# Two transformer layers on one core: the bias of the MLP's first product made by ScalarE, and another order of steps in a turn

## The chip, the core and the metric
The kernel runs on one core of a Trainium2 chip. Its time is the device time in microseconds of one execution; the median of three is 1187.67 us.

## The reference
An input x (2048 tokens of width 256, 32 sequences of 64) goes through four blocks, all in fp32:

```
x = offset_attention(x, ctx)
for layer in (1, 2):
    x += self_attention(layernorm(x))            # 16 heads of 16
    x += cross_attention(layernorm(x), ctx)
    x += gelu(layernorm(x) @ w1 + b1) @ w2 + b2  # w1: 256 x 1024
x = recurrent_block(x, state)
```
The change lies in the two layers.

## The kernel before
The tokens are cut into 4 groups of 512, each of 4 tiles of 128 tokens (2 sequences). The two layers are 8 **turns** (TURNS = 2 layers x 4 groups). A turn n works on 8 attention tiles k, 0 to 3 self-attention and 4 to 7 cross-attention of group n, and in the gaps on the MLP of the turn before (`prev`) and on the entry of the next one (`nxt`: layernorm, queries, keys, values). Turn 0 has no `prev`, turn 7 no `nxt`; 1 to 6 are one loop body. Each engine has a `turn` function of its own, a list written out by hand; an engine runs its list strictly in order, and semaphores join the engines.

One tile k goes like this. TensorE: `scores` (L976). VectorE: `mask`, a product with the mask (L1349). GpSimd: `add_mask` (L787). VectorE: `maximum` (L1356), `subtract` (L1361). ScalarE: `exps` (L1207). TensorE: `probs_T`, 8 transposes (L986). ScalarE: `copy_pT` (L1212). TensorE: `times_v` (L1001). VectorE: `normalize` (L1367, L1369). TensorE: `result_T` (L1009). ScalarE: `copy_cT` (L1217). TensorE: `out_project` (L1022). VectorE: `residual` with the layernorm's statistics (L1378 to L1385). GpSimd: `inv_std` (L792). VectorE: `norm` (L1390). Names with `next_` are one or two tiles ahead, names with `last_` one behind.

The MLP: `norm_T_mlp` (TensorE, L913), `norm_out(2)` (ScalarE, L1172), eight `hidden(j)` (TensorE, 512 wide, L1039) into two PSUM banks in turn, `pre(j)`, which adds b1 and empties the bank (VectorE, L1407), `gelu` in two halves of four (ScalarE, L1225), four `mlp_out(p)` (TensorE, L1053), `result(p)` (VectorE, L1399). `hidden(j)` for j from 2 to 5 waits for `pre(j - 2)`. The middle layernorm of a tile: `norm_T_mid` (L900), `norm_out_mid` (L1180), `queries_mid` (L957, L1192). Cross keys and values: `keys_ctx` and the entry's queries and keys (L870), `keys` (ScalarE, L1200), `values_ctx` and `values_in` (L880), `values` (VectorE, L1332). The entry: `stats_in` and `norm_in` (VectorE, L1308 to L1323), `queries_in` (ScalarE, L1187). `add_bias` and `add_bias_in` (GpSimd, L764 to L780) add row biases; `cross_masks` (L1340) prepares the masks.

SyncE's list holds the loads and stores. The x load of turn n + 2 waits for `add_bias_in` and `norm_in` of turn n + 1, and in turns 2 to 4 the second layer's weights are loaded in the same list, in parts, as the first layer's come free: the middle set (cross-attention's keys, values and queries) stands behind the x load in turn 3.

## Time and profile before

| what | value |
|---|---|
| median of 3 runs | 1187.67 us (1187.09 to 1188.38) |
| the profiled execution | 1188.55 us, span 1186.8 us |
| TensorE busy | 1050.7 us, 89% |
| VectorE busy | 815.3 us, 69% |
| ScalarE busy | 509.0 us, 43% |
| GpSimd busy | 434.1 us, 37% |
| mean granted clock | 0.961 |

Busy shares are of the whole span; the two layers take from about 110 to 819 us of it. A busy TensorE has matmuls in flight, at the clock then granted (1 is 2.4 GHz, 0.5 is 1.2 GHz). In the groups below, "idle before" is the time in which an engine stood before such an instruction, and the arrow names whose result ended it.

### The profile page before, as it was taken

Reading aid. Unit: us, or ns where it says so; the run is one execution under the profiler, and the core shown is the slowest. Engines: PE = TensorE matmul, PEld = TensorE weight load, DVE = VectorE, ACT = ScalarE, POOL = GpSimd, SP = SyncE. Lnnn points to the kernel's source line nnn. Section 1 sums busy time; section 2 is a strip of 40 time slices with the busy share of each in tenths; the row PEclk is TensorE's granted clock in tenths of the full one; section 3 lists DMA queues with packets and bytes.
Section 4 is the critical chain, followed back from the end, with each engine's and each line's share of the span. In section 5 each row is a group of like instructions: output and inputs, shape, how many; then the busy total and the mean of one; then the engine's idle time right before and its main releaser. Section 6 shows DMA issues by size and latency. Waiting matters only on the chain. (4 is left out here: it accounts for less than half of the span.)

```text
span 1186.8 us, 23743 instructions
## 1 busy us (share of the span) xinstructions
PE 1050.7 (89%) x9056; PEld 714.6 (60%) x9056; DVE 815.3 (69%) x1573; ACT 509.0 (43%) x954; POOL 434.1 (37%) x387
## 2 busy tenths in 40 slices
PE   7988786999999999999999999978996988888866
PEld 5876565668668668668668668656363353443524
DVE  3654776776776776776776866862448787796864
ACT  4643353464364363363373373461231434414331
POOL 2111443442442442442343343331307427264250
PEclk9988888999999999999999999989998999999988
DMA  7130100001002002102101000030000010010100
GB/s 252 62 94 23 41 1 19 24 2 38 24 2 74 23 2 82 36 2 77 55 6 33 24 18 20 9 115 18 1 27 30 1 36 21 0 38 0 36 1 18
DMA packets 38005, 41.14 MB, mean 35 GB/s; under 512 B 8640, under 2 KB 33536, under 8 KB 37648
## 3 DMA queue, kind: packets, MB, share of 16 engines
q1 hardware_dynamic: 37776, 39.54, 10.5%
q8 instruction: 82, 1.34, 0.5%
q14 instruction: 19, 0.16, 0.0%
q0 software_dynamic: 128, 0.10, 0.0%
HBM read 31.25 MB, written 8.39 MB: 33 GB/s over the span
## 5 line engine op out<-in xcount | busy, mean ns | idle before, releaser
L1356 DVE TENSOR_REDUCE b_neg_max<-head_area 128x16 f32<-128x1024 f32 x64 | 77.9, 1218 | 113.9 <-POOL head_area L787 113.5
L2104 POOL TENSOR_TENSOR c_rs<-c_st,head_area 128x512 f32<-128x512 f32 x64 | 88.6, 1416 | 96.8 <-DVE c_st L2583 95.9
L792 POOL TENSOR_TENSOR b_rstd<-b_var,minus_half 128x1 f32<-128x1 f32 x63 | 34.5, 548 | 241.4 <-DVE b_var L1385 241.4
L1207 ACT ACTIVATE head_area<-head_area 128x1024 f32<-128x1024 f32 x64 | 67.9, 1060 | 112.3 <-DVE head_area L1361 111.7
L1039 PE MATMUL ps<-b_hT_mlp,wl 128*128 128x512 f32 x224 | 108.3, 606 | 8.7 <-DVE b_act_g L1407 8.6
L1053 PE MATMUL ps<-w,b_act_g 128*128 128x256 f32 x448 | 104.4, 387 | 2.9 <-ACT b_act_g L1225 2.9
L787 POOL TENSOR_TENSOR head_area<-head_area,b_self_add 128x1024 f32<-128x1024 f32 x32 | 76.7, 2396 | 80.0 <-DVE head_area L1349 80.0
L787 POOL TENSOR_TENSOR head_area<-head_area 128x1024 f32<-128x1024 f32 x32 | 75.5, 2359 | 75.7 <-DVE head_area L1349 75.7
L1212 ACT ACTIVATE head_area<-ps 128x512 f32<-128x512 f32 x128 | 69.9, 598 | 72.5 <-PE ps L986 72.5
L1053 PEld LDWEIGHTS ps<-w,b_act_g 128*128 128x128 f32 x448 | 84.2, 193 | 15.6 <-ACT b_act_g L1225 3.0
L870 PE MATMUL ps<-head_area,wl 128*128 128x512 f32 x176 | 85.5, 609 | 0.0
L986 PE MATMUL ps<-ident,head_area 128*128 128x128 f32 x512 | 72.1, 287 | 12.7 <-DVE head_area L1349 11.8
L1361 DVE TENSOR_TENSOR head_area<-head_area,b_neg_max 128x1024 f32<-128x1024 f32 x64 | 78.1, 1220 | 1.2
L2583 DVE TENSOR_TENSOR_SCAN c_st<-head_area,ps 128x512 f32<-128x512 f32 x64 | 73.6, 1201 | 2.8 <-ACT ps L2391 2.8
L986 PEld LDWEIGHTS ps<-ident,head_area 128*128 128x128 f32 x512 | 60.6, 147 | 23.5 <-DVE head_area L1349 14.0
L1022 PE MATMUL ps<-wl,b_cT 128*128 128x256 f32 x252 | 70.1, 403 | 1.4 <-ACT head_area L1192 1.4
L1039 PEld LDWEIGHTS ps<-b_hT_mlp,wl 128*128 128x128 f32 x224 | 38.7, 190 | 45.7 <-issue 27.5
L1217 ACT ACTIVATE b_cT<-ps 128x256 f32<-128x256 f32 x64 | 24.5, 383 | 96.5 <-PE ps L1009 96.5
L880 PE MATMUL ps<-wl,head_area 128*64 128x128 f32 x1024 | 65.1, 282 | 0.0
L880 PEld LDWEIGHTS ps<-wl,head_area 128*64 128x64 f32 x1024 | 57.6, 141 | 9.1 <-issue 9.1
L1022 PEld LDWEIGHTS ps<-wl,b_cT 128*128 128x128 f32 x252 | 46.6, 201 | 13.9 <-issue 6.7
L870 PEld LDWEIGHTS ps<-head_area,wl 128*128 128x128 f32 x176 | 31.6, 193 | 24.9 <-issue 24.1
(262 smaller groups left out, 2213.1 us busy)
## 6 DMA issues: line engine op xcount, KB each, us to landing
head_area<-x_mid SPq DMA_DIRECT2D x9, 512.0 KB, 3.8
wl<-in_wl SPq DMA_DIRECT2D x4, 1024.0 KB, 6.8
head_area<-in_ctxT SPq DMA_DIRECT2D x8, 512.0 KB, 3.6
x_mid<-b_x_out SPq DMA_DIRECT2D x8, 512.0 KB, 3.6
area<-in_wc SPq DMA_DIRECT2D x1, 2336.0 KB, 8.5
a_x_in<-in_x SPq DMA_DIRECT2D x16, 128.0 KB, 2.9
a_y_in<-in_ctx SPq DMA_DIRECT2D x16, 128.0 KB, 3.4
w<-in_w SPq DMA_DIRECT2D x2, 1024.0 KB, 9.4
```

The lines of the kernel that those rows point to most:

```text
L787: pool.tensor_tensor(t, t, m.unsqueeze(1).broadcast_to([P, NH, S]), ALU.add).then_inc(add_ok, 1)
L870: mm = pe.matmul(ps[:, YB + c, :], weight(name, k, first + c * P, first + (c + 1) * P), rhs[:, k, :], start=(k == 0), stop=(k == NC - 1))
L880: mm = pe.matmul(ps[odd * S:(odd + 1) * S, YB + half, b * P:(b + 1) * P], lhs[:, k, t:t + S], weight(name, k, odd * P, (odd + 1) * P), sta ...
L986: mm = pe.transpose(ps[:, PT + half, i * P:(i + 1) * P], sc[:, k % 2, half, 2 * i:2 * i + 2, :].rearrange("q i k -> q (i k)"), w["ident"][ ...
L1022: mm = pe.matmul(ps[:, CO, OUT], cT[:, half, p * P:(p + 1) * P], weight(("ao", "co")[a], half), start=(half == 0), stop=(half == 1))
L1039: mm = pe.matmul(ps[:, YB + j % 2, :], weight("w1", k, j * P, (j + 1) * P), hT_mlp[:, k, :], start=(k == 0), stop=(k == NC - 1))
L1053: mm = pe.matmul(ps[:, YB + MLP_BANK[p], 0:D], act_g[:, j, p * P:(p + 1) * P], w["w2"][:, j, :], start=(j == 0), stop=(j == NJ - 1))
L1212: act.activation(pT[:, b, :, :].rearrange("k i q -> k (i q)"), ps[:, PT + b, :], ACT.Copy).then_inc(pT_ok, 1)
L1356: dve.tensor_reduce(neg_max[:, k % 2, :], t, AX, ALU.max, negate=True).then_inc(max_ok, 1)
L1361: dve.tensor_tensor(t, t, neg_max[:, k % 2, :].unsqueeze(2).broadcast_to([P, 2 * NPAIR, S]), ALU.add).then_inc(sub_ok, 1)
L2104: pool.tensor_tensor(rs[:, i % BUFS, :], st[:, i % 3, :], rF[:, i // RS, :], ALU.mult).then_inc(rs_ok, 1)
L2583: dve.tensor_tensor_scan(st[:, i % 3, :], decay[:, i // RS, :, :].rearrange("f b t -> f (b t)"), ps[:, VB[i % 4], :], 0.0, ALU.mult, ALU.a ...
```

## The change
`pre` goes from VectorE's list to ScalarE's, as an Identity activation with the bias; all four `turn` lists are put in another order. No other instruction is written in or taken out.

```diff
--- before.py
+++ after.py
@@ -812,41 +812,41 @@
             def turn(n, prev, nxt, entry_of=None):
                 last_inv_std(n, 0, prev)
+                add_bias(prev, 6)
                 next_add_mask(n, 0, nxt)
-                add_bias(prev, 6)
                 last_inv_std(n, 1, prev)
-                inv_std_in(nxt if entry_of is None else entry_of)
+                add_bias_in(nxt, 0)
                 next_add_mask(n, 1, nxt)
                 add_bias(prev, 7)
+                inv_std_in(nxt if entry_of is None else entry_of)
                 last_inv_std(n, 2, prev)
+                add_bias_in(nxt, 1)
                 next_add_mask(n, 2, nxt)
-                add_bias(n, 0)
-                add_bias_in(nxt, 0)
+                add_bias_in(nxt, 2)
                 last_inv_std(n, 3, prev)
                 next_add_mask(n, 3, nxt)
+                add_bias(n, 0)
                 add_bias(n, 1)
-                add_bias_in(nxt, 1)
                 last_inv_std(n, 4, prev)
                 next_add_mask(n, 4, nxt)
                 add_bias(n, 2)
-                add_bias_in(nxt, 2)
+                add_bias(n, 3)
+                next_add_mask(n, 5, nxt)
                 last_inv_std(n, 5, prev)
-                next_add_mask(n, 5, nxt)
-                add_bias(n, 3)
-                add_bias_in(nxt, 3)
-
-                last_inv_std(n, 6, prev)
                 next_add_mask(n, 6, nxt)
                 add_bias(n, 4)
+                last_inv_std(n, 6, prev)
+                add_bias_in(nxt, 3)
+
                 last_inv_std(n, 7, prev)
+                add_bias(n, 5)
                 next_add_mask(n, 7, nxt)
-                add_bias(n, 5)
             add_mask(0, 0)
             add_mask(0, 1)
@@ -1068,39 +1068,40 @@
             def turn(n, prev, nxt):
+                keys_ctx(n, 0, prev)
+
                 probs_T(n, 0, nxt)
                 last_project(n, 0, prev)
-                keys_ctx(n, 0, prev)
                 times_v(n, 0)
                 next_scores(n, 0, nxt)
                 keys_ctx(n, 1, prev)
                 result_T(n, 0)
                 values_ctx(n, 0)
+                last_project(n, 1, prev)
                 probs_T(n, 1, nxt)
-                last_project(n, 1, prev)
                 values_ctx(n, 1)
                 times_v(n, 1)
                 next_scores(n, 1, nxt)
                 norm_T_mlp(prev, n)
+                norm_T_mid(n, 0)
                 result_T(n, 1)
-                norm_T_mid(n, 0)
                 hidden(prev, 0, nxt)
                 queries_mid(n, 0)
                 probs_T(n, 2, nxt)
                 last_project(n, 2, prev)
-                hidden(prev, 1, nxt)
                 times_v(n, 2)
                 next_scores(n, 2, nxt)
+                hidden(prev, 1, nxt)
                 hidden(prev, 2, nxt)
-                hidden(prev, 3, nxt)
                 result_T(n, 2)
                 norm_T_mid(n, 1)
-
-                probs_T(n, 3, nxt)
+                hidden(prev, 3, nxt)
                 queries_mid(n, 1)
                 hidden(prev, 4, nxt)
+
+                probs_T(n, 3, nxt)
                 last_project(n, 3, prev)
                 times_v(n, 3)
                 next_scores(n, 3, nxt)
@@ -1108,45 +1109,45 @@
                 result_T(n, 3)
                 norm_T_mid(n, 2)
                 norm_T_in(nxt, prev)
+
                 probs_T(n, 4, nxt)
-
                 queries_mid(n, 2)
                 queries_in(nxt, 0)
                 last_project(n, 4, prev)
                 times_v(n, 4)
                 next_scores(n, 4, nxt)
                 queries_in(nxt, 1)
+                keys_in(nxt, 0)
+                norm_T_mid(n, 3)
+
+                probs_T(n, 5, nxt)
                 result_T(n, 4)
-                norm_T_mid(n, 3)
-                keys_in(nxt, 0)
+                keys_in(nxt, 1)
                 queries_mid(n, 3)
-
-                probs_T(n, 5, nxt)
-                last_project(n, 5, prev)
-                keys_in(nxt, 1)
+                hidden(prev, 6, nxt)
                 times_v(n, 5)
                 next_scores(n, 5, nxt)
-                hidden(prev, 6, nxt)
+                hidden(prev, 7, nxt)
+                last_project(n, 5, prev)
                 result_T(n, 5)
-                hidden(prev, 7, nxt)
                 probs_T(n, 6, nxt)
-                last_project(n, 6, prev)
                 values_in(nxt, 0, prev)
                 times_v(n, 6)
                 next_scores(n, 6, nxt)
+                last_project(n, 6, prev)
+                result_T(n, 6)
                 mlp_out(prev, 0, nxt)
-                result_T(n, 6)
+
+                probs_T(n, 7, nxt)
                 mlp_out(prev, 1, nxt)
-
-                probs_T(n, 7, nxt)
                 last_project(n, 7, prev)
+                times_v(n, 7)
                 values_in(nxt, 1, prev)
-                times_v(n, 7)
                 next_scores(n, 7, nxt)
                 mlp_out(prev, 2, nxt)
+                mlp_out(prev, 3, nxt)
                 result_T(n, 7)
-                mlp_out(prev, 3, nxt)
             scores(0, 0)
             for half in range(2):
@@ -1216,6 +1217,14 @@
                 act.wait_ge(c_ps, tile(n, k) + 1)
                 act.activation(cT[:, :, p * P:(p + 1) * P], ps[:, CX, CT].rearrange("f (h q) -> f h q", h=2), ACT.Copy).then_inc(c_ok, 1)
+            def pre(n, j):
+                if n is None:
+                    return
+                if j == 0:
+                    act.wait_ge(ready["hidden"], n + 1)
+                act.wait_ge(hid_ps, NJ * n + j + 1)
+                act.activation(act_g[:, j, :], ps[:, YB + j % 2, :], ACT.Identity, bias=vec("b1", j)).then_inc(pre_ok, 1)
+
             def gelu(n, half):
                 if n is None:
                     return
@@ -1233,52 +1242,60 @@
             def turn(n, prev, nxt):
                 copy_pT(n, 0)
+                keys(1, n, 0)
+                keys(1, n, 1)
+                copy_cT(n, 0)
                 next_exps(n, 0, nxt)
-                keys(1, n, 0)
-                copy_cT(n, 0)
-                keys(1, n, 1)
                 copy_pT(n, 1)
-                next_exps(n, 1, nxt)
                 norm_out(2, prev)
                 norm_out_mid(n, 0)
                 copy_cT(n, 1)
-
+                next_exps(n, 1, nxt)
                 queries_mid(n, 0)
+
                 copy_pT(n, 2)
+                pre(prev, 0)
+                pre(prev, 1)
+                norm_out_mid(n, 1)
+                pre(prev, 2)
+                pre(prev, 3)
+                copy_cT(n, 2)
                 next_exps(n, 2, nxt)
-                norm_out_mid(n, 1)
-                copy_cT(n, 2)
-
                 queries_mid(n, 1)
+
                 copy_pT(n, 3)
                 next_exps(n, 3, nxt)
-                gelu(prev, 0)
+                pre(prev, 4)
+                pre(prev, 5)
                 norm_out_mid(n, 2)
+                norm_out(0, nxt)
                 copy_cT(n, 3)
-                norm_out(0, nxt)
-
                 queries_mid(n, 2)
+
                 copy_pT(n, 4)
+                next_exps(n, 4, nxt)
                 queries_in(nxt, 0)
-                next_exps(n, 4, nxt)
                 queries_in(nxt, 1)
+                keys(0, nxt, 0)
                 norm_out_mid(n, 3)
                 copy_cT(n, 4)
+                copy_pT(n, 5)
                 queries_mid(n, 3)
-                copy_pT(n, 5)
-                keys(0, nxt, 0)
+                keys(0, nxt, 1)
                 next_exps(n, 5, nxt)
-                keys(0, nxt, 1)
+                gelu(prev, 0)
+                pre(prev, 6)
                 copy_cT(n, 5)
+                pre(prev, 7)
                 copy_pT(n, 6)
                 gelu(prev, 1)
                 next_exps(n, 6, nxt)
+
+                copy_pT(n, 7)
                 copy_cT(n, 6)
-
-                copy_pT(n, 7)
                 next_exps(n, 7, nxt)
                 copy_cT(n, 7)
@@ -1398,14 +1415,6 @@
                 dve.wait_ge(bias_ok[2], NP * n + p + 1)
                 dve.tensor_tensor(x_out[:, p, :], ps[:, YB + MLP_BANK[p], 0:D], x_mlp[:, p, :], ALU.add).then_inc(out_ok, 1)
-            def pre(n, j):
-                if n is None:
-                    return
-                if j == 0:
-                    dve.wait_ge(ready["hidden"], n + 1)
-                dve.wait_ge(hid_ps, NJ * n + j + 1)
-                dve.tensor_scalar(act_g[:, j, :], ps[:, YB + j % 2, :], vec("b1", j), None, ALU.add).then_inc(pre_ok, 1)
-
             def next_maximum(n, k, nxt):
                 if k + 1 < TILES:
                     maximum(n, k + 1)
@@ -1438,79 +1447,72 @@
             def turn(n, prev, nxt, entry_of=None):
-                next_maximum(n, 0, nxt)
-                next_subtract(n, 0, nxt)
+                cross_masks(n)
                 last_residual(n, 0, prev)
                 normalize(n, 0)
+
+                next_maximum(n, 0, nxt)
                 last_norm(n, 0, prev)
+                next_subtract(n, 0, nxt)
                 next_mask(n, 0, nxt)
-                cross_masks(n)
+                values(1, n, 0)
+                last_residual(n, 1, prev)
                 next_maximum(n, 1, nxt)
-                values(1, n, 0)
+                values(1, n, 1)
+                last_norm(n, 1, prev)
+                normalize(n, 1)
                 next_subtract(n, 1, nxt)
-                last_residual(n, 1, prev)
-                values(1, n, 1)
-                normalize(n, 1)
-                last_norm(n, 1, prev)
                 next_mask(n, 1, nxt)
                 stats_in(nxt if entry_of is None else entry_of)
+                last_residual(n, 2, prev)
+                next_mask(n, 2, nxt)
+                last_norm(n, 2, prev)
+                normalize(n, 2)
                 next_maximum(n, 2, nxt)
-                pre(prev, 0)
                 next_subtract(n, 2, nxt)
-                last_residual(n, 2, prev)
-                pre(prev, 1)
-                normalize(n, 2)
-                last_norm(n, 2, prev)
-                next_mask(n, 2, nxt)
-                pre(prev, 2)
+
+                next_maximum(n, 3, nxt)
                 norm_in(nxt if entry_of is None else entry_of)
-
-                next_maximum(n, 3, nxt)
-                pre(prev, 3)
                 next_subtract(n, 3, nxt)
                 last_residual(n, 3, prev)
-                pre(prev, 4)
                 normalize(n, 3)
                 last_norm(n, 3, prev)
-                pre(prev, 5)
                 next_mask(n, 3, nxt)
                 next_maximum(n, 4, nxt)
                 next_subtract(n, 4, nxt)
                 last_residual(n, 4, prev)
+                next_mask(n, 4, nxt)
+                last_norm(n, 4, prev)
                 normalize(n, 4)
-                last_norm(n, 4, prev)
-                next_mask(n, 4, nxt)
                 next_maximum(n, 5, nxt)
                 next_subtract(n, 5, nxt)
+                normalize(n, 5)
+                next_mask(n, 5, nxt)
                 last_residual(n, 5, prev)
-                normalize(n, 5)
-                last_norm(n, 5, prev)
-                next_mask(n, 5, nxt)
-                pre(prev, 6)
                 next_maximum(n, 6, nxt)
-                pre(prev, 7)
                 next_subtract(n, 6, nxt)
-                last_residual(n, 6, prev)
-                last_norm(n, 6, prev)
-                values(0, nxt, 0)
                 normalize(n, 6)
                 next_mask(n, 6, nxt)
+                values(0, nxt, 0)
                 result(prev, 0)
+                last_residual(n, 6, prev)
+                result(prev, 1)
                 next_maximum(n, 7, nxt)
-                result(prev, 1)
+                last_residual(n, 7, prev)
                 next_subtract(n, 7, nxt)
-                last_residual(n, 7, prev)
-                last_norm(n, 7, prev)
+                normalize(n, 7)
                 values(0, nxt, 1)
-                normalize(n, 7)
                 next_mask(n, 7, nxt)
                 result(prev, 2)
+                last_norm(n, 5, prev)
+                last_norm(n, 6, prev)
+                last_norm(n, 7, prev)
                 result(prev, 3)
             dve.wait_ge(ready["first"], 1)
```

## Rows read from the trace of the kernel before

**Rows 1.** Windows: length, busy us of PE, PEld, DVE, ACT, POOL, clock, DMA.
```profile
110.23:202.07 91.84, 72.08 (x948) 56.04 (x949) 65.76 (x119) 34.37 (x61) 36.23 (x31) 0.83 0.07 21
...
291.87:380.24 88.37, 84.11 (x929) 61.08 (x929) 63.54 (x128) 43.38 (x68) 32.73 (x29) 1.00 0.11 33
...
732.16:819.32 87.16, 76.94 (x778) 56.19 (x776) 56.25 (x120) 37.06 (x59) 25.32 (x24) 0.94 0.15 49
202.07:732.16 530.09, 505.72 (x5568) 367.84 (x5569) 381.22 (x761) 259.97 (x408) 199.41 (x176) 1.00 0.09 29
```

**Rows 2.** Waits of PE, turns 1 to 6: total, times, longest.
```profile
PE ps L1039 <- DVE b_act_g L1407: 7.6, 12, 1.1
PE ps L1009 <- DVE head_area L1369: 7.5, 6, 1.3
PE ps L913 <- DVE head_area L1332: 4.9, 6, 0.8
PE ps L986 <- DVE head_area L1349: 3.6, 7, 0.8
```

**Rows 3.** Groups by form, one turn (307.97 to 396.33): busy us, mean ns, idle before.
```profile
L1356 DVE TENSOR_REDUCE b_neg_max<-head_area 128x16 f32<-128x1024 f32 x8 | 9.7, 1218 | 13.9 <-POOL head_area L787 13.8
L1407 DVE TENSOR_SCALAR b_act_g<-ps,vl 128x512 f32<-128x512 f32 x8 | 5.9, 743 | 0.4 <-PE ps L1039 0.4
...
L1212 ACT ACTIVATE head_area<-ps 128x512 f32<-128x512 f32 x16 | 8.7, 598 | 10.1 <-PE ps L986 10.1
L1207 ACT ACTIVATE head_area<-head_area 128x1024 f32<-128x1024 f32 x8 | 8.5, 1061 | 11.5 <-DVE head_area L1361 11.4
...
L1225 ACT ACT_TABLE_LOAD x2 | 2.6, 1283 | 0.0
L1207 ACT ACT_TABLE_LOAD x2 | 2.6, 1283 | 0.0
...
L1187 ACT ACTIVATE area<-ps,vl 128x512 f32<-128x512 f32 x2 | 1.4, 687 | 1.5 <-PE ps L870 1.4
```

**Rows 4.** Waits of PE, turn 0.
```profile
PE ps L1009 <- DVE head_area L1369: 10.5, 6, 3.9
PE ps L986 <- DVE head_area L1349: 6.8, 4, 4.6
```

**Rows 5.** Waits of PE, turn 7.
```profile
PE ps L1053 <- ACT b_act_g L1225: 2.9, 1, 2.9
```

**Rows 6.** Timeline of PE, start of turn 2: start, length, instruction.
```profile
291.87 1.09 PE L986 MATMUL ps<-ident,head_area 128*128 128x128 f32 x8 [0.42 <-issue]
292.80 1.03 PE L1022 MATMUL ps<-wl,b_cT 128*128 128x256 f32 x4
293.66 1.88 PE L870 MATMUL ps<-head_area,wl 128*128 128x512 f32 x4
295.47 1.13 PE L1001 MATMUL ps<-area,head_area 128*64 128x34 f32 x32
296.53 0.69 PE L976 MATMUL ps<-area 32*64 32x128 f32 x32
```

**Rows 7.** Timeline of GpSimd and VectorE, turn 2.
```profile
322.68 2.36 POOL L787 TENSOR_TENSOR head_area<-head_area 128x1024 f32<-128x1024 f32 x1 [2.23 <-DVE head_area L1349]
...
323.17 3.80 DVE L1323 TENSOR_SCALAR xc_in<-head_area,mv_in,rstd_in 128x256 f32<-128x256 f32 x4
```

**Rows 8.** Timeline of VectorE, tiles 6 and 7 of turn 0.
```profile
183.60 1.22 DVE L1356 TENSOR_REDUCE b_neg_max<-head_area 128x16 f32<-128x1024 f32 x1 [2.47 <-POOL head_area L787]
...
190.32 1.21 DVE L1349 TENSOR_TENSOR head_area<-ps,b_self_mul 128x1024 f32<-128x1024 f32 x1
194.00 1.22 DVE L1356 TENSOR_REDUCE b_neg_max<-head_area 128x16 f32<-128x1024 f32 x1 [2.47 <-POOL head_area L787]
```

**Rows 9.** Timeline of SyncE, turn 3.
```profile
445.44 0.37 SPq L680 DMA_DIRECT2D wl<-in_wl  x1
```

**Rows 10.** Windows: ten us of turn 0.
```profile
150.00:160.00 10.00, 7.85 (x44) 6.17 (x44) 9.77 (x15) 3.79 (x9) 4.46 (x4) 0.51 0.00 0
```

## The prediction, made before the change was measured

> **What bounds the kernel.** I read the windows of the two-layer stage first, turn by turn. A turn is the work between two starts of TensorE's transposes of tile 0. Six of the eight turns (1 to 6) are alike: together 530.09 us, TensorE busy 505.72 us of it at granted clock 1.00, VectorE 381, ScalarE 260, GpSimd 199; one of them is 88.37 us with TensorE busy for 84.11 [rows 1]. So TensorE bounds these turns, and what a new order can win in them is at most its idle time, 24.4 us or 4.1 us a turn. Turn 0, which has no MLP to fill holes, is different: 91.84 us, TensorE busy 72.08, mean clock 0.83. Turn 7, with no next group, takes 87.16 us with 76.94 busy at 0.94 [rows 1]. The stages before and after (the first 110 us, and the last 367) are not touched.
>
> Then TensorE's waits, to see who ends them. In turns 1 to 6 all are for VectorE [rows 2]: hidden products for the bias `pre` (7.6 us, 12 times), `result_T` for `normalize` (7.5), `norm_T_mlp` for the second `values` (4.9), `probs_T` for the mask product (3.6). VectorE isn't full; it is late because it works in program order and stands still elsewhere: 13.9 us of a turn it waits in front of `maximum` for GpSimd's `add_mask` [rows 3]. Nothing waits for ScalarE there. In turn 0 the waits are 10.5 us for `normalize` and 6.8 us for masks, one of them 4.6 us [rows 4]; in turn 7 the longest is 2.9 us for the second gelu [rows 5].
>
> **Bias to ScalarE.** Per turn 8 operations of 743 ns leave VectorE, 5.9 us. ScalarE's form of the same work is its Identity with a bias on the same 128x512, 687 ns, so it gains 8 x 0.69 = 5.5 us [rows 3]. ScalarE goes from 43.4 us busy in 88.4 [rows 1] to 48.9, less what follows. The row is the same kind of operation with the same shape, so both bounds of the price are close: 0.69, or 0.74 if it is no better than VectorE. The Trainium skill ("ScalarE: Activation LUTs", rules for kernel authors) says to put an add on VectorE and not on ScalarE. By that rule the move would be a loss on the unit cost. Here the source is PSUM in fp32 and the rows have ScalarE 0.06 us cheaper; the sum goes by the rows.
>
> **Two table loads less.** Before, exps stand between the two gelus, so a turn has 2 + 2 loads of 1283 ns [rows 3]. After, `gelu(prev, 0)` and `gelu(prev, 1)` have only Identity and Copy between them, which take no load in the kernel before when they follow a gelu. That leaves 1 + 1, and gives back 2.6 us of ScalarE: net +2.9 us, about 46 us busy a turn (52%). The same page (what a table load costs) puts 1.38 us of draining beside each load, 2.66 us a switch, so 5.3 us given back by it; the rows show the load alone, and ScalarE isn't the bound either way.
>
> **The order, walked through a steady turn.** I laid the new lists beside each other with start-to-start lengths from TensorE's rows [rows 6]: `probs_T` 0.93, a projection 0.86 to 0.95, `times_v` 1.06, `scores` 0.65, a 512-wide product 1.8; VectorE's large operations 1.2, exp 1.06, two `copy_pT` 1.1 to 1.2 [rows 3]; a residual with its statistics 1.3 and `add_mask` 2.4, both estimates from the loop in [rows 8]. Time 0 is the start of `keys_ctx(n, 0)`.
> - Head. `keys_ctx(0)` to 1.7 covers the last mask product and exp; `probs_T(0)` to 2.7, projection 3.6, `times_v(0)` 4.7, scores 5.3, `keys_ctx(1)` 7.0. VectorE: `residual(n, 7)` now comes first and waits until 3.8, `normalize(0)` is done at 5.8, well ahead of `result_T(0)`; `maximum(1)` and `subtract(1)` end at 8.6. ScalarE: `keys(1, n, 1)` waits until 7.1 with `copy_cT(0)` and exp of tile 1 queued behind it, done at 10.0. TensorE gets to `probs_T(1)` at 10.1. No stall, but the slack is 0.1 us.
> - The MLP's entry. `values(1, n, 1)` is done at about 15.0; `norm_T_mlp` begins at 14.7 and needs it at 15.1. The 0.8 us stall of before goes. `hidden(0)` waits for the second `norm_out` until about 16.7: a new stall of 0.5.
> - Hidden products. `pre(0)` is done at 21.8, `hidden(2)` is reached at 24.7; `pre(1)` at 25.5, `hidden(3)` at 26.9; likewise for 4 and 5. The 1.3 us a turn behind `pre` goes.
> - Middle. `norm_in` moves to where GpSimd rests. Before, its four operations took 3.80 us, beside an `add_mask` that began just before it [rows 7]; undisturbed I take 1.7. `normalize(3)` is done at 35.2 and `result_T(3)` is reached at 36.6: 1.25 us goes. Mask of tile 5 is done at 36.9, `probs_T(4)` is reached at 37.9: 0.5 goes.
> - End. Exp of tile 6 to 55.2, load and gelu to 58.4, `pre(6)` to 59.1: `values_in(0)`, reached at 58.9, waits 0.3. The second gelu ends at 63.3, `mlp_out(0)` is reached at 64.05. VectorE waits for `mlp_out` results with slack.
>
> Left are some 1.0 us of new stalls and small latencies; I take 1.1 against 4.1 us, **3.0 us a turn, 18 us for six turns**. Bounds: all idle gone, 24; half kept, 12; none, 0.
>
> **Turn 0.** In its last tiles VectorE runs a strict loop: maximum, subtract, residual, norm, values, normalize, mask, then GpSimd's addition before the next maximum. Two maxima stand 10.40 us apart, with the mask's start 6.72 us after the first; after the mask VectorE stands 2.47 us for the addition [rows 8]. The new order puts `normalize` and the mask ahead of residual and values, so these run beside the addition: 1.2 + 1.2 + 0.7 + 1.2 + 2.4 = 6.8 us, and then other chains (projection, copies, values) hold it near 8. Walking on from the first scores, `keys_ctx(0)` fills 1.8 us of the 4.6 us hole; `probs_T(2)` comes 3 us earlier than before, `probs_T(4)` 6 us, turn 1's tile 0 12 us, and then `keys_ctx` is already done. I take **13 us**. Bounds: 20, the idle time of the window (19.8), and 5, the opening and one tile. The clock's missing 0.17 I leave as it is.
>
> **Turn 7.** 10.2 us idle and some cold products. The same cures apply up to tile 5 (about 3 us of stalls); the shorter chain at tiles 4 to 6 wins 3 to 4. Against it, the chain exp, gelu, `pre(6)`, copies, gelu still has 8 us in a row on ScalarE, and `mlp_out(0)` keeps a stall of 2 to 3 us. `result_T(7)` is now last, so its copy (0.4 us) is no longer covered before all engines meet, +0.3. My walk ends 8 us earlier: **8 us**, bounds 3 and 11.
>
> **Queues.** SyncE's list is unchanged but what it waits for moves. `add_bias_in(nxt, 3)` goes behind `inv_std(n, 5)` on GpSimd, at about 70.6 of the turn. In turn 3 the x load and then the middle weights of layer 2 wait behind it. Before, the weights' first load was issued at 445.44 [rows 9], and turn 4 begins at about 468.5 (380.24 + 88.3) [rows 1]: 23 us. After, it is issued at about 71.5 of a turn of 85; a load of this kind I take at 8 us, so some 5 us of slack are left, and the first product of turn 4 now needs these weights. I cost it at nothing; if it slips it costs the slip once. `cross_masks` is earlier, the mask load with it: no cost.
>
> **Sum.** The profiled execution took 1188.55 us, its span is 1186.8, and the median of the runs is 1187.67, 0.9 lower. 1188.55 - 18 - 13 - 8 + 0.3 = 1149.9; by the median **1149 us**, 3.2% less.
>
> **Rivals.**
> - *The stalls only move* (chance 0.2). ScalarE's list now has in-order waits for TensorE (keys, `pre(1)`, `pre(3)`, `pre(5)`) with exps behind them; the 0.1 us of slack at `probs_T(1)` speaks for it, ScalarE's load of 52% to 55% against it. Steady turns keep 3 of 4.1 us and turns 0 and 7 give 14: 1187.67 - 6 x 1.1 - 14 = 1167.
> - *TensorE full everywhere* (0.1): 24 + 18 + 10 gone: 1136.
> - *Slower* (0.03): one mechanism, exp behind `keys(1, n, 1)` and the `pre`s. Each of the eight tiles would wait longer for its exp on TensorE. Turns 0 and 7 give 14 to 21 anyway, so it decides from a wait of 4.1 + 18/6 = 7.1 us a turn, 0.9 us for each tile. At 1.3 us a tile, 10.4 a turn, it gives 1187.67 + 6 x 6.3 - 18 = 1207.5. Against it: no wait for ScalarE in [rows 2], and 1.1 us in my walk.
> - *The change does nothing to measure* (0.03): the removed VectorE time was never on the path, and turn 0 is held by something the waits don't name: 1186 to 1190.
> - *The clock falls* (0.04). In 10 us of turn 0 with transposes, short products and small holes the granted clock was 0.51, near its lower level of 1.2 GHz, though TensorE was busy for 7.85 us [rows 10]. Turn 0's work at the full level is about 72.08 x 0.83 = 60 us; if the new order held it at a mean of 0.6 it would take 100 us, with 6 idle 106, so 14 us more than before instead of 13 less: 1187.67 - 18 - 8 + 14 = 1176. [...] Against it: fewer and shorter holes, and stretches of the same turn at 1.00.
>
> **Chances.** Forecast 0.6, the others as said. A measurement of this kernel can tell 0.2% from none. Faster 0.94, same 0.03, slower 0.03. The range takes the bounds of the three terms together with the first two rivals: 1136 to 1168.
>
> **What would show it.** TensorE's waits for the bias at `hidden` gone, and no other of over 0.5 us a turn in turns 1 to 6; a steady turn of 85 to 85.8 us; 7 + 7 table loads where there were 14 + 14; `norm_in` near 1.7 us; VectorE near 58 us a turn, ScalarE 46; turn 0 near 79 us and turn 7 near 79. Wrong would be waits of TensorE for exp above 1 us a turn, or a steady turn over 87.

## The result, and the profile after

After the change the kernel takes 1134.25 us (median of 4 runs, 1130.38 to 1135.84), against 1187.38 us before (4 runs, 1185.45 to 1188.38): ratio 0.955, 95% interval 0.9523 to 0.9577. The forecast was 1149 with a range from 1136 to 1168: the sign is right, the size too small, and the result lies 2 us outside the range. The profiled execution took 1134.52 us, 54.0 less than the profiled one of before.

The head of its page:

```profile
span 1132.7 us, 23729 instructions
...
PE 1030.0 (91%) x9056; PEld 707.2 (62%) x9056; DVE 768.0 (68%) x1517; ACT 517.4 (46%) x996; POOL 440.2 (39%) x387
```

TensorE's busy time fell from 1050.7 to 1030.0 us, though it has the same work. That is the first sign of what the forecast missed.

The windows of turns 0, 1, 6 and 7 and of turns 1 to 6 together, cut as in [rows 1] (length, busy PE, PEld, DVE, ACT, POOL, clock, DMA):

```profile
111.21:189.71 78.50, 67.89 (x952) 51.25 (x953) 61.96 (x117) 33.83 (x61) 36.86 (x32) 0.91 0.08 24
189.71:274.00 84.29, 83.15 (x929) 61.39 (x930) 60.21 (x124) 44.67 (x74) 36.17 (x30) 1.00 0.07 21
...
608.40:690.92 82.52, 82.52 (x929) 61.44 (x928) 57.03 (x119) 44.55 (x74) 33.74 (x29) 1.00 0.06 19
690.92:765.13 74.21, 69.20 (x774) 52.56 (x772) 48.26 (x109) 38.33 (x65) 25.30 (x24) 1.00 0.17 56
189.71:690.92 501.21, 496.80 (x5568) 368.67 (x5569) 345.74 (x719) 267.45 (x444) 204.82 (x175) 1.00 0.10 31
```

| part | before | after | gain | forecast |
|---|---|---|---|---|
| turn 0 | 91.84 | 78.50 | 13.3 | 13 |
| turns 1 to 6 | 530.09 | 501.21 | 28.9 | 18 |
| turn 7 | 87.16 | 74.21 | 13.0 | 8 |

The three gains make 55.2 us; the stage before the layers is 1.0 longer (first scores at 111.21 instead of 110.23). The cuts are not quite fair to turns 0 and 7: the first `keys_ctx` of a turn used to stand behind the cut and now stands ahead of it, so turn 0 holds one more product of this kind and turn 7 one less (952 and 774 matmuls instead of 948 and 778). Cut at the start of that `keys_ctx` (187.58 and 689.21), the gains are 15.5, 28.5 and 11.2 us. In turns 1 to 6 the gain has two parts: idle time of TensorE fell from 24.4 to 4.4 us (501.21 - 496.80), which is 20.0, and its **busy** time from 505.72 to 496.80, which is 8.9, with the same 5568 matmuls. Turn 6 takes 82.52 us and has no hole at all.

TensorE's waits of turns 1 to 6, beside [rows 2]: from 23.6 us in four rows (31 waits) to 4.4 (7 waits). Then the first two of turn 0, beside [rows 4]:

```profile
PE ps L870 <- issue: 1.9, 1, 1.9
PE ps L870 <- DVE b_x_out L1416: 1.8, 3, 0.6
PE ps L986 <- DVE head_area L1366: 0.4, 2, 0.2
PE ps L1009 <- DVE head_area L1386: 0.3, 1, 0.3
```
```profile
PE ps L986 <- DVE head_area L1366: 3.9, 3, 2.7
PE ps L1009 <- DVE head_area L1386: 2.9, 3, 2.4
```
The waits for `pre` and `values` are gone, and those for `normalize` and the masks are down to 0.3 and 0.4 us. What is new is `keys_ctx` (L870) at the head of a turn: three times 0.6 us behind the last `result` (L1416), and once 1.9 us for nothing that the profile names. In turn 7 the wait for the second gelu at `mlp_out` [rows 5] is gone.

The groups of one turn (524.98 to 608.40), beside [rows 3]; lines have moved by some 15:

```profile
L1373 DVE TENSOR_REDUCE b_neg_max<-head_area 128x16 f32<-128x1024 f32 x8 | 9.7, 1211 | 4.1 <-POOL head_area L787 4.1
L1407 DVE TENSOR_SCALAR b_xc<-b_x_cur,b_mv,b_rstd 128x256 f32<-128x256 f32 x8 | 4.0, 521 | 0.1
L1340 DVE TENSOR_SCALAR xc_in<-head_area,mv_in,rstd_in 128x256 f32<-128x256 f32 x4 | 1.4, 402 | 0.0
```
```profile
L1226 ACT ACTIVATE b_act_g<-ps,vl 128x512 f32<-128x512 f32 x8 | 5.5, 688 | 5.9 <-PE ps L1039 5.9
...
L1234 ACT ACT_TABLE_LOAD x1 | 1.3, 1283 | 0.0
L1208 ACT ACT_TABLE_LOAD x1 | 1.3, 1283 | 0.0
```

VectorE stands 4.1 us in front of `maximum` instead of 13.9: it now has other work to do while GpSimd adds the mask. `pre` costs ScalarE 688 ns, `norm_in` 1.4 us for its four instead of 3.8, and a turn has one load of each table instead of two. A switch to the other table, in ScalarE's timeline:

```profile
576.43 1.07 ACT L1208 ACTIVATE head_area<-head_area 128x1024 f32<-128x1024 f32 x1
577.51 1.28 ACT L1234 ACT_TABLE_LOAD   x1
578.81 1.91 ACT L1234 ACTIVATE b_act_g<-b_act_g 128x2048 f32<-128x2048 f32 x1
```

The exp ends at 577.50, the load follows at once, the gelu 0.02 us behind it. So a switch costs 1.3 us here. The 1.38 us of draining that the Trainium skill ("ScalarE: Activation LUTs", what a table load costs) puts beside it doesn't show; two loads less a turn gave ScalarE 2.6 us, as the forecast's sum had it, not 5.3. (The experiment late_gelu_only below shows it alone: over five turns ScalarE is busy for 203.72 us instead of 216.60, so 2.6 us a turn.)

In turn 0 the two maxima that [rows 8] shows of before, and SyncE's load of the middle weights, beside [rows 9]:

```profile
176.08 1.22 DVE L1373 TENSOR_REDUCE b_neg_max<-head_area 128x16 f32<-128x1024 f32 x1 [1.27 <-POOL head_area L787]
...
182.86 1.21 DVE L1373 TENSOR_REDUCE b_neg_max<-head_area 128x16 f32<-128x1024 f32 x1
```
```profile
427.32 0.37 SPq L680 DMA_DIRECT2D wl<-in_wl  x1
```

These two maxima stand 6.8 us apart, where it was 10.4 and the forecast said near 8. It isn't the whole loop: the maxima around them are 9.1 us before and 11.9 us behind (166.94 and 194.78), so over three intervals the gain is 2.7 us (30.6 to 27.8). The load of the weights is issued 12.9 us before the product that needs them (`keys_ctx` of turn 4, at 440.23) and the last load of the set has landed by about 434.1; the product waits for `result` and not for it.

### The profile page after: what moved, and what is told of

Its sections match the earlier page's. It is cut to its first block and busy times, and to the rows that moved or that the text cites. A ratio compares the mean times of both kernels' runs of the same rounds, so it can differ in the third digit from the quotient of the medians.

```text
span 1132.7 us, 23729 instructions
## 1 busy us (share of the span) xinstructions
PE 1030.0 (91%) x9056; PEld 707.2 (62%) x9056; DVE 768.0 (68%) x1517; ACT 517.4 (46%) x996; POOL 440.2 (39%) x387
## 3 DMA queue, kind: packets, MB, share of 16 engines
q1 hardware_dynamic: 37776, 39.54, 10.9%
## 5 line engine op out<-in xcount | busy, mean ns | idle before, releaser
L1039 PE MATMUL ps<-b_hT_mlp,wl 128*128 128x512 f32 x224 | 107.0, 605 | 0.0
L1053 PE MATMUL ps<-w,b_act_g 128*128 128x256 f32 x448 | 100.9, 381 | 0.0
L1053 PEld LDWEIGHTS ps<-w,b_act_g 128*128 128x128 f32 x448 | 83.4, 190 | 11.6 <-issue 1.0
L792 POOL TENSOR_TENSOR b_rstd<-b_var,minus_half 128x1 f32<-128x1 f32 x63 | 40.8, 648 | 124.9 <-DVE b_var L1402 124.2
L870 PE MATMUL ps<-head_area,wl 128*128 128x512 f32 x176 | 84.5, 609 | 3.9 <-issue 1.9
L1378 DVE TENSOR_TENSOR head_area<-head_area,b_neg_max 128x1024 f32<-128x1024 f32 x64 | 80.4, 1256 | 1.2
L986 PE MATMUL ps<-ident,head_area 128*128 128x128 f32 x512 | 68.4, 278 | 5.3 <-DVE head_area L1366 4.3
L986 PEld LDWEIGHTS ps<-ident,head_area 128*128 128x128 f32 x512 | 59.5, 143 | 16.5 <-issue 8.9
L880 PE MATMUL ps<-wl,head_area 128*64 128x128 f32 x1024 | 62.6, 275 | 0.0
L1039 PEld LDWEIGHTS ps<-b_hT_mlp,wl 128*128 128x128 f32 x224 | 38.6, 190 | 34.5 <-issue 31.3
L880 PEld LDWEIGHTS ps<-wl,head_area 128*64 128x64 f32 x1024 | 55.3, 137 | 4.0 <-issue 4.0
L1226 ACT ACTIVATE b_act_g<-ps,vl 128x512 f32<-128x512 f32 x56 | 38.5, 688 | 41.2 <-PE ps L1039 41.2
L870 PEld LDWEIGHTS ps<-head_area,wl 128*128 128x128 f32 x176 | 30.8, 192 | 32.9 <-issue 30.4
```

Source lines behind the costliest of these rows:

```text
L870: mm = pe.matmul(ps[:, YB + c, :], weight(name, k, first + c * P, first + (c + 1) * P), rhs[:, k, :], start=(k == 0), stop=(k == NC - 1))
L880: mm = pe.matmul(ps[odd * S:(odd + 1) * S, YB + half, b * P:(b + 1) * P], lhs[:, k, t:t + S], weight(name, k, odd * P, (odd + 1) * P), sta ...
L986: mm = pe.transpose(ps[:, PT + half, i * P:(i + 1) * P], sc[:, k % 2, half, 2 * i:2 * i + 2, :].rearrange("q i k -> q (i k)"), w["ident"][ ...
L1039: mm = pe.matmul(ps[:, YB + j % 2, :], weight("w1", k, j * P, (j + 1) * P), hT_mlp[:, k, :], start=(k == 0), stop=(k == NC - 1))
L1053: mm = pe.matmul(ps[:, YB + MLP_BANK[p], 0:D], act_g[:, j, p * P:(p + 1) * P], w["w2"][:, j, :], start=(j == 0), stop=(j == NJ - 1))
L1378: dve.tensor_tensor(t, t, neg_max[:, k % 2, :].unsqueeze(2).broadcast_to([P, 2 * NPAIR, S]), ALU.add).then_inc(sub_ok, 1)
```

## The experiments

A steady turn is given below as the mean of the five spacings between the stores of turns 1 to 6 in the profiled execution: 88.17 us before, 83.56 after. Waits are TensorE's from 250 to 690 us. Ratios are to the kernel before, on the same chip.

**The bias alone.** The order of before; `pre` goes to ScalarE, at the places that its neighbours allow:

```diff
                 copy_pT(n, 2)
+                pre(prev, 0)
                 next_exps(n, 2, nxt)
+                pre(prev, 1)
+                pre(prev, 2)
+                pre(prev, 3)
...
                 next_exps(n, 3, nxt)
+                pre(prev, 4)
                 gelu(prev, 0)
+                pre(prev, 5)
```


> The order of before, with the bias made by ScalarE where its operands are ready (pre 0 after the copies of tile 2, 1 to 3 after the next exp, 4 and 5 around the first gelu, 6 and 7 around the last copy of tile 5). Theory A (the order is the change; the bias only gives it room): the waits of TensorE for the bias go (1.3 us shown a turn, some 1.5 with what is hidden in busy time), the others stay, 0.990, some 1175 us. Theory B (VectorE's 5.9 us a turn were the cause of all its lateness): waits for normalize and for the masks go too, steady turns of 84 us, 0.972 or less, under 1155 us.

1186.9 us, ratio 1.0003 (0.9983 to 1.0023), a turn 88.72. Its waits:

```profile
PE ps L894 <- ACT b_act_g L1225: 10.4, 5, 2.1
PE ps L913 <- DVE head_area L1348: 4.1, 5, 0.8
PE ps L1039 <- ACT b_act_g L1225: 2.8, 5, 0.6
```

The waits for `normalize` (L1009) and for masks (L986) are gone, as theory B had it, but the time isn't: `norm_T_in` (L894) waits 2.1 us in every turn for `pre(5)`, which stands behind the gelu and its table load. Neither theory foresaw that. Less work for VectorE is real, and with these places for `pre` it is worth nothing.

**The order alone.** The new lists; `pre` stays on VectorE, beside the same neighbours (`pre(0)` behind the mask of tile 4, which is `next_mask(n, 2)`, and so on):

```diff
                 next_mask(n, 2, nxt)
+                pre(prev, 0)
                 last_norm(n, 2, prev)
                 normalize(n, 2)
+                pre(prev, 1)
```


> The new order, with the bias on VectorE. Theory A: it has most of the gain, steady turns of 84 to 85 us against 83.5 in the changed kernel, turn 0 as in the changed kernel, 1140 to 1148 us. Theory B: VectorE is as late as before, steady turns of 87 to 88, and only turn 0 keeps its gain: 1165 to 1175 us.

1150.77 us, ratio 0.9693 (0.9676 to 0.9711), a turn 86.16. That is nearer to theory A, but slower than the 84 to 85 us a turn that it named. Its first waits:

```profile
PE ps L894 <- DVE b_act_g L1408: 3.3, 5, 0.7
PE ps L1009 <- DVE head_area L1370: 2.8, 5, 0.6
```

So the order is worth 3.1% and the bias, placed as above, 0.0% alone; both together 4.5%. On top of the new order the bias brings 2.6 us a turn and 1.4% in all. Turn 0, which has no `pre`, takes 77.2 us here (108.09 to 185.27), so its gain is the order's alone.

**The place of the first gelu.** Three kernels: in the order of before with `pre` on ScalarE, the first gelu moved behind the exp and keys of tile 5 (bias_late_gelu); the same move with `pre` left on VectorE (late_gelu_only); and from the kernel after, the gelu put back to the early place (gelu_early). From bias_late_gelu:

```diff
-                gelu(prev, 0)
+                pre(prev, 4)
+                pre(prev, 5)
                 norm_out_mid(n, 2)
...
                 keys(0, nxt, 1)
+                gelu(prev, 0)
+                pre(prev, 6)
```


> The order of before with the bias on ScalarE, and the first gelu behind exp and keys of tile 5, so that one table load of each kind is left a turn. bias_alone lost at the bias of product 5, which I had put behind the first gelu (2.1 us a turn). If that was the whole loss, the waits for the bias now stay away and the time is 2.5 us a turn less: 1170 to 1176 us. If the order of before has no use for the freed VectorE time (theory A), other waits take up part of it: 1176 to 1184 us. If ScalarE is now late for keys or values: over 1187.

> Before, with the bias on VectorE, and only ScalarE's first gelu moved behind exp and keys of tile 5. bias_late_gelu against bias_alone was 3.3 us a turn. If the place of that gelu is worth this by itself (a wait of TensorE for the layernorm copies that the trace books elsewhere, and one pair of table loads less), steady turns of 85.5 to 86.5 us and 1165 to 1175 us. If the gelu only hurt where the bias stood behind it, nothing: 1183 to 1189 us, since before shows no wait of TensorE for ScalarE.

> The changed kernel with the first gelu straight behind the bias of product 5, as before: 2 + 2 table loads a turn again. It puts 3.2 us and one exp-table load ahead of the layernorm copies and of the next exp. If ScalarE's order has slack, 1134 to 1138 us; if it is tight at queries_mid(2) and norm_out(0), waits of 2 to 3 us a turn, 1148 to 1160 us.

bias_late_gelu: 1164.84 us, ratio 0.979 (0.9731 to 0.9849), a turn 85.38, and the wait of 2.1 us at L894 is gone. late_gelu_only: 1187.41 us, ratio 0.9995 (0.9979 to 1.0011), a turn 88.18, with 5 + 5 table loads from 250 to 690 us where before has 10 + 10. gelu_early: 1162.09 us, ratio 0.9784 (0.9743 to 0.9825), a turn 86.74; its first wait:

```profile
PE ps L957 <- ACT head_area L1181: 11.9, 5, 2.4
```

Two table loads less are worth nothing to measure while VectorE is late; the move of the bias is worth nothing while the gelu stands in its way; together they give 2.1%, somewhat more than expected. So nearly half of the 4.5% can be had in the order of before, and the other lists add the rest. In the new order the early gelu costs 3.2 us a turn, of which TensorE shows 2.4 as a wait of `queries_mid` (L957) for the layernorm copies that stand behind the gelu.

**One engine back.** From the kernel after: TensorE's list of before (old_pe); TensorE's and ScalarE's, the latter with `pre` as in bias_late_gelu (new_dve_pool); VectorE's and GpSimd's (old_dve_pool). The start of old_pe:

```diff
-                keys_ctx(n, 0, prev)
-
                 probs_T(n, 0, nxt)
                 last_project(n, 0, prev)
+                keys_ctx(n, 0, prev)
```


> The changed kernel with TensorE's list as before. Theory A with the gain in TensorE's own order: waits of 2 us a turn or more come back, 1150 to 1160 us. Rival: the other three engines' lists give the gain, TensorE's list is near indifferent: 1134 to 1140 us.

> VectorE's and GpSimd's lists new, TensorE's and ScalarE's as before (ScalarE with the bias as in bias_late_gelu). If the gain lies in VectorE not standing before the maximum, it is here alone: 1150 to 1165 us. If the lists only work as a set (as TensorE's old list with three new ones gave 1245 us): slower than before, 1200 to 1260 us.

> The reverse: TensorE's and ScalarE's lists new, VectorE's and GpSimd's as before. Serial loop of 10.4 us at every tile against TensorE's 10.4 us a tile: waits for normalize and masks come back. As a set theory: 1200 to 1260 us. If the gain was in TensorE's list: 1150 to 1165 us.

old_pe: 1245.24 us, ratio 1.0483 (1.0429 to 1.0537), a turn 96.96. new_dve_pool: 1271.79 us, 1.0704 (1.0665 to 1.0742), 99.64. old_dve_pool: 1257.66 us, 1.0582 (1.0545 to 1.062), 98.3. The first was expected at 1134 to 1160 us, the third is in its range, the second a little above it. Waits of old_pe, then of old_dve_pool:

```profile
PE ps L986 <- ACT head_area L1207: 16.4, 8, 3.4
PE ps L957 <- ACT head_area L1180: 11.2, 5, 2.2
```
```profile
PE ps L1009 <- DVE head_area L1386: 34.7, 14, 4.5
```

In new_dve_pool the longest wait is that of hidden products (L1039) for `pre` on ScalarE, 19.0 us in all and up to 4.7 at a time. Each mixture is slower than both whole sets. There is no list that carries the gain: an in-order engine whose neighbours come in another order waits for them, with everything behind it.

**The mask ahead of residual and norm, in the order of before.** Only VectorE's slots 4 to 7 change (the last two alike, with `values` too):

```diff
                 next_subtract(n, 4, nxt)
-                last_residual(n, 4, prev)
                 normalize(n, 4)
-                last_norm(n, 4, prev)
                 next_mask(n, 4, nxt)
+                last_residual(n, 4, prev)
+                last_norm(n, 4, prev)
```


> Before, and on VectorE alone, in tiles 4 to 7, normalize and the next mask ahead of residual, norm and values. If the serial loop of VectorE and GpSimd is what lengthens turn 0's last tiles, two maxima there stand about 8 us apart and not 10.4, and turn 0 is 6 to 8 us shorter; steady turns within 1 us of before: 1178 to 1182 us. If other chains hold turn 0, it stays at 91 us and the time at 1187.

1288.59 us, ratio 1.0858 (1.084 to 1.0876), a turn 102.7. Turn 0 is not shortened: 92.1 us (106.67 to 198.79) against 91.8, and its last maxima stand 9.9 and 10.0 us apart (184.45, 194.30, 204.29), not 8, since the norms there take 2.4 us each. The two longest waits of the steady turns, then VectorE and GpSimd at the same time:

```profile
PE ps L1053 <- DVE area L1332: 23.7, 8, 3.1
PE ps L900 <- DVE b_xc L1390: 17.7, 5, 3.5
```
```profile
384.71 2.42 DVE L1390 TENSOR_SCALAR b_xc<-b_x_cur,b_mv,b_rstd 128x256 f32<-128x256 f32 x1 [0.67 <-POOL b_rstd L792]
```
```profile
384.64 2.34 POOL L787 TENSOR_TENSOR head_area<-head_area,b_self_add 128x1024 f32<-128x1024 f32 x1
```

This is the worst kernel of all, by a move that the full change makes too. This norm starts inside `add_mask` and takes 2.42 us, to 0.15 us behind its end; over the turns norms take 1415 ns on average, where a turn of the kernel before has 407: 8 us more of VectorE in a turn. The full change differs in two ways that may guard it: the last three norms are put off to the end of the turn, and TensorE asks for the values later. No run tests them one by one. The first is not complete: the norms of a turn of the kernel after still take 521 ns on average, one of them 1.33 us.

**`norm_in` beside `add_mask`.** From the kernel after:

```diff
                 next_mask(n, 2, nxt)
+                norm_in(nxt if entry_of is None else entry_of)
                 last_norm(n, 2, prev)
...
                 next_maximum(n, 3, nxt)
-                norm_in(nxt if entry_of is None else entry_of)
```


> The changed kernel with norm_in straight behind the mask of tile 4, so that it runs beside GpSimd's add_mask, as before. If VectorE's scale-and-shift from SBUF is held while GpSimd adds, its four operations take 3.4 to 4 us and not 1.4; result_T(2) then waits some 2 us a turn: 1140 to 1150 us. If VectorE's slack hides it: 1132 to 1136 us with the operations still long.

1156.63 us, ratio 0.9724 (0.9692 to 0.9756), a turn 85.92. Its first wait, and its `norm_in`:

```profile
PE ps L1009 <- DVE head_area L1386: 10.1, 5, 2.0
```
```profile
304.01 3.40 DVE L1340 TENSOR_SCALAR xc_in<-head_area,mv_in,rstd_in 128x256 f32<-128x256 f32 x4
```
```profile
304.17 2.45 POOL L787 TENSOR_TENSOR head_area<-head_area 128x1024 f32<-128x1024 f32 x1 [0.28 <-DVE head_area L1366]
```

Four operations take 3.40 us instead of 1.4, and `result_T` (L1009) waits the difference of 2.0 us in every turn, as expected. The time is above the expected range; turn 0 is longer too, 83.4 us for 78.5, in part by the clock of its opening (see below). The first of the four starts ahead of the addition and takes 0.405 us; the second starts at 304.33, inside it, and takes 2.44, to 0.15 us behind its end; the other two take 0.40 each. The Trainium skill ("SBUF — State Buffer", who interferes with whom) says that a pair of ports is shared by VectorE and GpSimd, that `tensor_scalar` is among the operations that can ask for it, and that whoever has it first blocks the other for a whole instruction. The runs agree: 2.44 us here and 2.42 in the experiment before, each until just behind the addition's end.

**`result_T(7)` ahead of the last `mlp_out`**, from the kernel after:

```diff
                 mlp_out(prev, 2, nxt)
-                mlp_out(prev, 3, nxt)
                 result_T(n, 7)
+                mlp_out(prev, 3, nxt)
```


> The changed kernel with result_T(7) ahead of the last mlp_out, as before. It should give 0.3 us at the end of turn 7, where all engines meet, and nothing in steady turns: 1132 to 1135 us. If the 0.6 us that TensorE stands at the head of a turn is for the chain behind result_T(7), it goes too: 1129 to 1131 us.

1140.18 us, ratio 0.9586 (0.9559 to 0.9613). A steady turn is 83.41 against 83.56, so the place does nothing there. The profiled execution is 6.3 us longer in span; 4.7 of it stand ahead of the first store (276.58 against 271.86), of which 1.7 ahead of the first scores, where the two kernels don't differ, and 2.8 in turn 0, whose length scatters by as much (see below). The time is above what was expected, but this decides nothing: the intervals overlap.

**VectorE's late slots made serial again**, from the kernel after:

```diff
                 next_subtract(n, 5, nxt)
+                last_residual(n, 5, prev)
                 normalize(n, 5)
                 next_mask(n, 5, nxt)
-                last_residual(n, 5, prev)
```
(slot 6 alike, its first `values` with it)

> The changed kernel with VectorE's residuals of tiles 4 and 5 and the first values ahead of normalize and mask, in slots 5 and 6, as before. If the loop VectorE, GpSimd, VectorE sets turn 0's last tiles, turn 0 grows by 2 to 4 us. In steady turns TensorE's work is 10 us a tile: if that hides the loop, no wait there and 1136 to 1139 us; if not, waits for normalize or masks of 1 to 3 us a turn, 1142 to 1155 us.

1214.48 us, ratio 1.0213 (1.0153 to 1.0272), a turn 93.65. Its first wait, and the place in VectorE's timeline:

```profile
PE ps L1009 <- DVE head_area L1386: 27.4, 10, 3.5
```
```profile
340.64 1.23 DVE L1378 TENSOR_TENSOR head_area<-head_area,b_neg_max 128x1024 f32<-128x1024 f32 x1
349.25 0.42 DVE L1395 TENSOR_TENSOR b_x_cur<-ps,b_x_cur 128x256 f32<-128x256 f32 x1 [7.39 <-PE ps L1022]
```

VectorE stands 7.39 us in the residual, because the new TensorE list has put that projection behind both last hidden products; `normalize`, which is ready, stands behind it. The cost is 10.1 us a turn, far above the 1 to 3 that were expected: the old slots don't fit the new TensorE list. Turn 0, the first question of this run, takes 91.5 us (107.55 to 199.07), 13.0 more than in the kernel after, where 2 to 4 were expected; up to 2.8 of that is the clock of its opening, which differs from one execution to another (see below). So with the new lists around them, these two slots decide over most of what turn 0 has gained.

## Why the prediction was right in kind and too small in size

**Turns 1 to 6: the term that failed.** By the profiled executions the forecast was 15.4 us too high (1149.9 to 1134.52): 10.9 of it lie in these turns, 5.0 in turn 7. The step was "what a new order can win in them is at most its idle time, 24.4 us or 4.1 us a turn"; 28.9 us were won. The forecast for the idle time was close (18 expected, 20.0 gone). But the busy time of 84.11 was taken for a floor, and it isn't one: 8.9 us of busy time went as well, a term that the sum doesn't have. The same five groups in TensorE's timeline, first with two waits (before), then without (after):

```profile
329.24 1.98 PE L1039 MATMUL ps<-b_hT_mlp,wl 128*128 128x512 f32 x4
332.48 0.44 PE L1009 MATMUL ps<-ident,head_area 128*128 128x128 f32 x2 [1.25 <-DVE head_area L1369]
332.80 0.44 PE L900 MATMUL ps<-ident,b_xc 128*128 128x128 f32 x2
333.07 1.04 PE L894 MATMUL ps<-ident,xc_in 128*128 128x128 f32 x8
334.59 1.09 PE L986 MATMUL ps<-ident,head_area 128*128 128x128 f32 x8 [0.48 <-DVE head_area L1349]
335.52 1.06 PE L957 MATMUL ps<-head_area,wl 128*128 128x128 f32 x8
```
```profile
557.55 1.98 PE L1039 MATMUL ps<-b_hT_mlp,wl 128*128 128x512 f32 x4
559.37 0.38 PE L1009 MATMUL ps<-ident,head_area 128*128 128x128 f32 x2
559.59 0.38 PE L900 MATMUL ps<-ident,b_xc 128*128 128x128 f32 x2
559.81 1.16 PE L894 MATMUL ps<-ident,xc_in 128*128 128x128 f32 x8
560.81 1.04 PE L986 MATMUL ps<-ident,head_area 128*128 128x128 f32 x8
561.68 1.06 PE L957 MATMUL ps<-head_area,wl 128*128 128x128 f32 x8
```

From the first start to the last it is 6.28 us before and 4.13 after: 2.15 us less, of which the profile shows 1.25 + 0.48 = 1.73 as waits. The other 0.42, 0.21 for each wait, is counted as busy. Part lies ahead of the wait: unstalled, the next group starts 1.82 us after a hidden product whose length is given as 1.98, since one overlaps the other; with a wait it starts after 3.24, and 3.24 - 1.25 = 1.99. The rest lies behind it: the pair after the wait takes 0.32 to the next start instead of 0.22. That is one place. Whole windows of five turns (between the stores of turns 1 and 6) give a little more: the kernel before has 27 listed waits there and 420.84 us busy, bias_late_gelu 17 and 417.97, the kernel after 4 and 414.19; both differences come to 0.29 us a wait. From 31 waits to 7, at 0.21 to 0.29, is 5.0 to 7.0 us of the 8.9. About 1.0 more is in turn 1, whose window showed a clock of 0.98 before: 85.46 us busy, where the next turn had 84.11, against 83.15 and 82.78 after. The last 0.9 us or more stay open. Longer waits hide more: norm_in_early has 8 waits, five of them of 2.0 us, and 416.84 us busy, 0.66 for each of the 4 that the kernel after doesn't have.

So the floor lies below the busy time: turn 6, with no wait, takes 82.52 us, not 84.11. The start-to-start lengths with which the forecast walked the turn were the better basis. An estimate: the medians of the spacings without a wait, added up over the turn at 307.97 of the kernel before, make some 83 us.

With this the rival "TensorE full everywhere", taken from the idle times as well, had the same fault: it said 1136 with nearly no idle time left in the eight turns (52 of 54 us gone), and 1134 came out with 20.0 us still idle in them (10.6, 4.4 and 5.0). The lower end of the range was this rival's 1136. The forecast's own bounds for its three terms, 24, 20 and 11, add up to 55 us and would have given 1133; the result would then have been inside, by luck, since these bounds too count idle time alone.

**The stalls that were walked.** Waits for `pre` and `values` went, and all but 0.3 and 0.4 us of those for `normalize` and masks, as said. The new stalls feared (0.5 at `hidden(0)`, 0.3 at `values_in(0)`) are in no row; 1.1 us a turn was allowed and 0.7 shows, at other places. A steady turn is 83.5 (501.21 / 6) where 85 to 85.8 was forecast.

**ScalarE and VectorE.** 688 ns for `pre` (0.69), one pair of table loads a turn, ScalarE 44.6 us in a turn (46), VectorE 57.1 (58), `norm_in` 1.4 (1.7): right, or near. The parts run separately show what the walk didn't: the bias alone is worth nothing, because the gelu stands in the way.

**Turn 0**: 13.3 for 13, and this close only by luck. Idle time fell by 9.2 (19.8 to 10.6) and busy time by 4.2 at a mean clock of 0.91 for 0.83, which the forecast left as it was; and without the `keys_ctx` that has come into its window the gain is 15.5. The loop of the last tiles was summed as 6.8 (its terms make 6.7) and raised to near 8; 6.8 was measured, but 11.9 for the next interval. And the turn's length scatters from one execution to another: 89.9 to 92.9 us in four kernels that have the turn 0 of before (before, bias_alone, late_gelu_only, bias_late_gelu), 78.5 and 77.2 with that of after (after, gelu_early). Part of it is the clock in the opening: the first `values_in` take 6.06 us in the profiled execution of before and 3.71 in that of after, but 3.71 too in before_loop, which has the same lists up to there as before. The rival in which the clock falls went the other way: with less idle time the granted clock rose. In the ten us of [rows 10] (not the same instructions), then 0.51 with 7.85 busy, the kernel after has

```profile
150.00:160.00 10.00, 9.80 (x105) 7.79 (x104) 5.51 (x12) 5.73 (x12) 4.45 (x5) 0.78 0.01 2
```

**Turn 7**: 13.0 for 8, outside the bounds of 3 to 11; 11.2 with its first `keys_ctx`. Idle fell by 5.2 (10.2 to 5.0) and busy by 7.7. Of the busy time 1.7 is this `keys_ctx` (689.21 to 690.92), the clock (0.94 to 1.00) accounts for some 4.6 (an estimate, 76.94 x 0.06), and 1.4 stays open. The forecast named "some cold products" and gave them no price, and it kept a stall of 2 to 3 us at `mlp_out(0)` that didn't come.

**The load of the middle weights** did not slip: it was issued 12.9 us ahead, where 13.5 was reckoned, and had landed after 6.8 us, where 8 was, which leaves some 6 us of slack for the estimated 5.

## What to carry to other kernels

The idle time of the engine that bounds is not the most that a new order can win: each wait also hid some 0.2 to 0.3 us in the busy time here, and long holes cost clock. Take the floor from start-to-start spacings of instructions that nothing holds up. Hand-written lists of in-order engines are one object: measure an order as a whole, since half of a good one was 5 to 7% worse than none here, and a lighter engine paid only where the receiving engine's list had a place for the work that is not behind something long. Keep a `tensor_scalar` between SBUF tiles (here fp32, 128x256) away from a running GpSimd addition.

## What the runs showed of the hardware that was not expected

- A `tensor_scalar` on 128x256 in SBUF that starts inside a GpSimd addition ends 0.15 us behind it: up to 2.44 us for 0.41. One that starts just ahead of the addition takes its 0.405. Moving four of them by a few steps cost 2.4 us a turn (85.92 for 83.56).
- A table load costs ScalarE 1.28 us and nothing around it.
- Holes of TensorE cost twice when they are long: the granted clock falls behind them. Between the stores of turns 1 and 6 the windows of the kernel after and of the one with serial slots read

```profile
271.86:689.64 417.78, 414.19 (x4642) 307.59 (x4643) 285.65 (x596) 222.77 (x371) 168.64 (x145) 1.00 0.11 34
```
```profile
291.39:759.64 468.25, 434.88 (x4641) 321.23 (x4642) 285.75 (x596) 224.53 (x371) 168.09 (x145) 0.96 0.10 30
```
With the same matmuls TensorE is busy for 20.7 us more, at 0.96 of full clock; 414.19 / 0.96 would be 431, so most of it is the clock, and the rest is in the size of what its 18 listed waits hide. In one turn of the kernel with serial slots it can be seen: behind waits of 2.01 and 0.69 us the clock reads 0.50 from 353 to 355 us, and the 32 products of `values_in` take 2.67 us, 1.95 later in the turn. Behind a wait of 3.47 us it reads 0.50 from 363 to 365, and an `mlp_out` takes 4.86 us, the next one 3.62. The waits of the kernel before, up to 1.3 us, leave it at 1.00 in turns 2 to 6.
